# Loading first-layer expert weights in runs of 3072 bytes in place of 1536, in a graph-attention and mixture-of-experts kernel

## What is computed

```python
x = x + gnn(layernorm(x), edge_index, W1, a_src1, ..., b2)        # two attention layers
xf = layernorm(x)
combine = gw[:, :, None] * ew                                      # 2 of 4 groups, 4 of 8 experts
for g in range(G):                                                 # G = 4, 8 experts in each
    h = gelu(jnp.einsum('nd,edm->enm', xf, W1[g]) + b1[g][:, None, :], approximate=False)
    o = jnp.einsum('enm,emd->end', h, W2[g]) + b2[g][:, None, :]
    y = y + jnp.einsum('end,ne->nd', o, combine[:, g, :])
```

## Time and profile before

| | |
|---|---|
| runs | 1545.48, 1545.87, 1550.06 us; median 1545.87 |
| span of the profiled execution | 1547.4 us |
| TensorE busy (matmuls) | 1367.3 us, 88% |
| VectorE busy | 1158.1 us, 75% |
| ScalarE busy | 741.6 us, 48% |
| GpSimd busy | 493.7 us, 32% |
| DMA | 222.06 MB, mean 144 GB/s |
| hardware queue q1 (SyncE's) | 78690 packets, 140.50 MB, 28.3% of 16 engines |
| software queue q0 (GpSimd's) | 22240 packets, 78.63 MB, 24.9% of 16 engines |
| loads of expert weights | 192 of 384 KiB each, half of them first-layer |

### The profile page before, as it was taken

How to read it: one execution, slowest core, us unless ns; L and a number is a source line. 1 busy time by engine, 2 the same in 40 slices (tenths; PEclk the granted TensorE clock), 3 DMA queues, 4 the chain that set the end, 5 groups by cost and what they waited for, 6 DMA issues and landing times. The chain is left out here.

```text
span 1547.4 us, 30224 instructions
## 1 busy us (share of the span) xinstructions
PE 1367.3 (88%) x7686; PEld 1137.4 (74%) x7687; DVE 1158.1 (75%) x1817; ACT 741.6 (48%) x1175; POOL 493.7 (32%) x554
## 2 busy tenths in 40 slices
PE   6888988878778879799957999999999999999995
PEld 3656656733223339799956899999999999989895
DVE  5479999899999978858886566555565656787782
ACT  3465565255555553412214455444454545665662
POOL 1000000003333410032324445545555545454563
PEclk9999999799999989999977999999999999999998
DMA  4300002041222223144577888877788887999974
GB/s 168 136 10 17 17 14 74 17 176 60 72 93 72 68 59 128 57 124 114 124 206 249 212 231 223 185 182 170 178 210 202 211 203 181 238 282 283 248 163 83
DMA packets 101759, 222.06 MB, mean 144 GB/s; under 512 B 16551, under 2 KB 55719, under 8 KB 101586
## 3 DMA queue, kind: packets, MB, share of 16 engines
q1 hardware_dynamic: 78690, 140.50, 28.3%
q0 software_dynamic: 22240, 78.63, 24.9%
q10 hardware_dynamic: 784, 2.36, 0.4%
HBM read 161.78 MB, written 55.74 MB: 141 GB/s over the span
## 5 line engine op out<-in xcount | busy, mean ns | idle before, releaser
L972 PE MATMUL ps_o<-prob,h_head 128*97 128x512 f32 (+1 forms) x480 | 188.4, 530 | 51.2 <-DVE prob L914 51.2
L2022 POOL DMA_INDIRECT out_nodes<-y,to_index x92 | 153.4, 1667 | 217.4 <-DMA out_nodes<-y,to_index 194.1
L2307 PE MATMUL ps_h<-e_hi,e_xt_hi 128*128 (+1 forms) x546 | 195.7, 359 | 10.4 <-ACT e_xt_hi L2126 6.0
L2292 PE MATMUL ps_y<-e_hi,e_ht_hi 128*128 (+1 forms) x546 | 191.0, 350 | 9.7 <-issue 7.1
L972 PEld LDWEIGHTS ps_o<-prob,h_head 128*97 128x97 f32 x480 | 73.5, 165 | 165.5 <-issue 90.2
L2307 PE MATMUL ps_h<-e_lo,e_xt_hi 128*128 (+1 forms) x546 | 187.3, 343 | 0.0
L2292 PE MATMUL ps_y<-e_hi,e_ht_lo 128*128 (+1 forms) x546 | 183.7, 336 | 0.0
L2292 PE MATMUL ps_y<-e_lo,e_ht_hi 128*128 (+1 forms) x546 | 183.6, 336 | 0.0
L2190 DVE TENSOR_TENSOR e_lo<-raw,e_hi (+1 forms) x189 | 175.6, 953 | 6.2 <-ACT e_hi L2134 5.9
L2143 ACT ACTIVATE y<-ps_y,gate 128x768 f32 (+1 forms) x91 | 82.2, 904 | 170.1 <-PE ps_y L2292 160.4
L2011 POOL DMA_INDIRECT landing<-table,index x93 | 131.3, 1412 | 82.7 <-DVE in_rows L2242 48.1
(11 more groups left out here) (333 smaller groups left out, 3066.0 us busy)
## 6 DMA issues: line engine op xcount, KB each, us to landing
raw<-in_ew SPq DMA_DIRECT2D x192, 384.0 KB
w_room<-rel_dram SPq DMA_DIRECT2D x14, 640.0 KB, 4.7
b_all<-in_eb SPq DMA_DIRECT2D x32, 192.0 KB
al_src<-al_dram SPq DMA_DIRECT2D x1, 5000.0 KB, 14.7
xs<-in_x SPq DMA_DIRECT2D x5, 768.0 KB, 12.8
x_in_t<-in_x SPq DMA_DIRECT2D x10, 384.0 KB, 3.6
out_nodes<-x SPq DMA_DIRECT2D x10, 384.0 KB, 4.1
table<-xf SPq DMA_DIRECT2D x10, 384.0 KB, 2.6
```

The source lines that it names most:

```text
L972: turn = nc.tensor.matmul(ps_o[u][0:C1 + 1, c, 0:WID[c]], h_head[:, u, t, :], prob[:, t % 2, 512 * c:512 * c + WID[c]], start=(t == 0), st ...
L2022: nc.gpsimd.indirect_dma_start(out, bass.IndirectOffsetOnAxis(to_index[:, w:w + 1], 0), y[:, w, :], None, bounds_check=ROWS - 1, compute_o ...
L2292: last = nc.tensor.matmul(ps_y[:, half, 0:HALF], a, b[:, bass.ds(u, 1), at:at + HALF].rearrange("p o d -> p (o d)"), start=(m == 0), stop= ...
L2307: nc.tensor.matmul(ps_h[:, 0:HID], xt_hi[:, c, :], b[:, bass.ds(e % 2, 1), c * HID:(c + 1) * HID] .rearrange("p o m -> p (o m)"), start=(c ...
```

## The change

The host lays out W1 so that, for each expert and each partition, the six rows that the partition gets stand one after the other: 6 x 384 values, 9216 bytes. The input in HBM has the shape (32 x 128, 2304) in place of (32 x 768, 384). A load of a third takes 768 values out of each of 128 such rows: 3072 bytes for each partition, at a step of 9216 bytes in HBM. Slots, semaphores, waits, order and sizes of the loads stay, as does everything that reads `raw1`.

```diff
@@ -1867,9 +1867,8 @@
 def load_first(eng, s, w1, e, piece):
 
     at = piece * PIECE
-    eng.dma_start(s.raw1[:, bass.ds(e % WRING, 1), at:at + PIECE].rearrange("p o (k m) -> p (o k) m", m=HID),
-                  w1[bass.ds(e * D + piece * (D // 3), D // 3), :].rearrange("(k p) m -> p k m", p=P)) \
-       .then_inc(s.w1_in[piece], 16)
+    eng.dma_start(s.raw1[:, bass.ds(e % WRING, 1), at:at + PIECE].rearrange("p o m -> p (o m)"),
+                  w1[bass.ds(e * P, P), at:at + PIECE]).then_inc(s.w1_in[piece], 16)
@@ -2467,7 +2466,7 @@
-        "ew1": ffn["W1"].reshape(E * D, HID),
+        "ew1": ffn["W1"].reshape(E, KD, P, HID).swapaxes(1, 2).reshape(E * P, ROW),
```

## The result

The changed kernel is slower: 1552.83 us median (1547.82 to 1559.92) against 1544.75 us (1542.24 to 1550.06), 6 runs each, ratio 1.0051 with a 95% interval of 1.0027 to 1.0074. That is about 7.9 us, above the bound of 0.3%. 1545 us was forecast; 1552.83 lies just outside the range of 1537 to 1552 and on the other side of no change.

A forecast was written before the change was run, and what follows sets the result against it. The prediction took TensorE to bound the middle stretch, with loads mattering only in the two loose stretches. The profiled span of 1547.4 us less 1.05 us, set against the median, gave 1544.8, rounded 1545 us; range 1537 to 1552 us.

The forecast's parts named there:

- What bounds the kernel: Expert stage: TensorE bounds 866 to 1340 us, no load is late; loads matter only by lengthening scatters and gathers.
- none names a DMA: TensorE's waits in the loose stretches, 22.1 us idle: no releaser is a DMA; the largest with a releaser is ScalarE's e_xt_hi, 6.0 us.
- The bytes and packets: First-layer loads: same 37.7 MB, 12,288 packets fewer on the hardware queue, engine time 1.1 us per MB or 2% cheaper.
- The sum: Whole kernel: 1.05 us saved on 15.3 MB of loads in the two loose stretches, giving 1544.8, rounded 1545 us.
- The trace of before holds the price of the new form: First-layer loads take the second-layer load's form, so its traced 51.1 us per MB prices them, against 52.2 before.
- rival A: Scatters under first-layer bursts: half as many packets make them shorter, gaining 9 us, to 1537 us; chance 0.20.
- main case: Whole kernel: cheaper packets give 1545 us, itself between 1541.5 and 1549; chance 0.63.
- Rival B: Scatters under bursts: longer packets push in front, 0.54 us each, 7.0 us over 13 bursts, to 1553 us; chance 0.14.
- The tipping point: Scatter under a burst: longer packets pushing in front decide the time once it takes 9.0 us in place of 8.5.
- The rule of the Trainium skill: DMA engines change queues only after a whole packet; if descriptors are grouped so, the turn is 24.6 KB in both forms.
- C: Hardware queue: the transfer might be cut into 1536-byte runs anyhow, giving 1546 us; chance 0.03.
- The signs I named: Scatter under a burst near 8.5 us, near 7 or 9 for rivals; wrong if loose-stretch TensorE idle moves over 4 us.

The follow-up runs named there:

- f4_9216: The changed kernel's layout, but one load per expert for the whole first layer, 9216 contiguous bytes per partition; ratio 1.0109 to the kernel before.
- f3_second_1536: The kernel before with the second layer's loads also in runs of 1536 bytes, two per partition, out of contiguous blocks; ratio 1.0001 to the kernel before.
- h2_after_turns: The changed kernel, but SyncE issues first-layer and second-layer loads by turns for each third; ratio 0.9985 to the kernel before.
- f1_after_paced: The changed kernel, but SyncE issues each load of experts 2 to 31 only once the one before has landed; ratio 1.0720 to the kernel before.

## Why the prediction was wrong

**What bounds the kernel: half right.** TensorE is the bound of the middle stretch, no load is ever late, and the chain of scatters is the way by which a load can matter: all three hold in the profile after. Wrong was the weight given to "none names a DMA" in TensorE's waits. TensorE waits for in_rows (3.9 us before, all of it between 815 and 866 us), VectorE for the gate copy, and GpSimd's gate copy can stand behind a scatter. I read the last releaser and not the one behind it. The middle stretch, set at nothing, lost 2.0 us of TensorE's time in one trace of the changed kernel and nothing in the two others (idle 6.7, 3.9 and 3.3 us against 4.7), so setting it at nothing isn't refuted; the late stretch lost in all three (11.4, 12.9 and 13.4 us against 10.1).

**The bytes and packets: right, and beside the point.** 12,288 packets fewer, and the issue at 342 ns where 354 was expected. The hardware queue's share was to fall by 0.1 to 0.3 points and fell by 0.4, 0.8 and 0.5 in three traces, but kernels with the packets of before differ among themselves by 0.7, so this tests nothing. The sum turned a saving of 1.1 us per MB into 1.05 us of gain, though, as the prediction itself says, the saving is less than the spread of either group. f4_9216 shows the error: its queue has the lowest share with all bytes brought in time, 26.4%, and it is the slowest kernel with loads in time. Engine time per MB was the wrong currency for an edit whose only effect goes through what else waits at the engines.

**"The trace of before holds the price of the new form": the step that failed.** The second-layer load has the form of the new one, but is mostly issued alone; a first-layer load has two others on its heels. The prediction priced the new form by engine time alone, 1.05 us gained, and put the delay of the scatters by a burst of it at nothing; the runs showed 6.3 to 7.9 us lost. f3_second_1536 shows that in the second layer the size costs nothing, and h2_after_turns that it costs nothing in the first once the loads are apart. I had the two lines of the earlier trace rows and used them against rival A only. They counted against my main case as much: the scatter of 5.58 us under one long-run load says nothing on a scatter under three.

**Rival B was the case that happened**, at a chance of 0.14. Its price, 0.54 us for a scatter under a burst and 13 bursts in the loose stretches, 7.0 us, stands beside 0.5 us (9.07, 9.04, 9.06 against 8.55) and 6.3 to 7.9 us. The tipping point, 9.0 in place of 8.5 us, was passed just so. The agreement in the total is partly luck: the 13 bursts weren't seen to pay the full price each, and without gaps between the runs both are about half as large (8.78 and 8.86 us, 1.0022 and 1.0025). B's mechanism, one turn for each packet, has the direction right, and its size only at 3072 bytes: by strict turns 768 bytes should have made scatters shorter than 1536, and did not. A packet of 9216 bytes takes 347 ns and one of 1536 bytes 65 ns (medians), so eight turns would add 2.3 us to a scatter under f4_9216's loads; its 20 longest are 0.84 us longer. How a burst delays a scatter stays open.

**The rule of the Trainium skill** ("DMA: Bandwidth & Descriptors", section "Queues, rings and completion order"), that an engine drains a packet of typically 9 to 17 descriptors before it turns to another queue, spoke for B falling, since a piece has the same bytes on an engine in both forms. The runs with three loads issued together don't agree with that use of it: 3072 bytes cost 0.22 to 0.51%. The 1.09% of 9216 bytes doesn't speak against it, for there one load has three times the bytes on an engine, and its turn would be longer by that reading too. How descriptors are grouped on this queue no run here shows.

**Rival A** is refuted: half as many packets made the longest scatters longer. **C** too, by the packets. **The signs I named:** a scatter under a burst at 9 or more was B's sign and came; TensorE's idle in the two loose stretches moved by 0.1 us together (12.0 + 10.1 to 10.6 + 11.4), and by 0.9 and 1.9 us in the other two traces, so my test for being wrong did not even fire. Stretches fixed in time can't see a stage that grows by 4.1 us; the length from the first to the last h_in can.

**The range** was too narrow on the slow side by its own terms: it ended at the worst engine time per MB and left out most of B, which had been priced at 1553 us.

## What to carry to other kernels

A transfer that nobody waits for can still cost time: 13.4 us here, and it can only come through other work that it delays, the small, serial transfers first of all. Before making its runs longer, ask whether several such loads leave at once while a latency-bound DMA is under way, and look one releaser further back than the one the view of waits names. If they do, spread the issue first; here that took the whole loss of the longer runs away with a change in the order of two loops, and gained nothing for the shorter ones.

## What was unexpected of the hardware

A load of 393 KB, the only one of its queue under way, took 4.1 us (median) from issue to landing, and 180 one after the other cost 7.2% (f1_after_paced): a queue with one load in flight could not feed this stage, though in the kernel before the hardware queue filled only 28.3% of the engines' time. And scatters under loads had a floor that cutting runs did not lower: 8.55, 8.45 and 8.51 us for the 20 longest with runs of 1536, 1536 and 768 bytes.
